# Four row buffers in place of two for the edge pass of a graph network on one core

## The reference, cut to what matters

```python
row, col = edge_index[0], edge_index[1]
h = jnp.concatenate([x[row], edge_attr], axis=1) @ W1 + b1      # one row per edge
mu, var = jnp.mean(h, axis=0), jnp.var(h, axis=0)               # over all edges
h = (h - mu) * jax.lax.rsqrt(var + EPS) * gamma + beta
msg = h * jax.nn.sigmoid(h)
sums = jax.ops.segment_sum(msg, col, num_segments=N)
```

## Time and profile before

| | us |
|---|---|
| median of 3 executions (9289.38 to 9297.74) | 9289.8 |
| the profiled execution: its own time | 9297.53 |
| its span in the trace | 9295.6 |
| edge pass in it, first gather to last add | 1831.93 to 4319.14 |
| mean granted TensorE clock over the span | 0.772 of full |

### The profile page before, as it was taken

One profiled execution on the slowest core, in us unless ns is written; L12 is line 12 of the kernel. 1 busy time (PEld: TensorE's weight loads), 2 busy tenths in 40 slices (PEclk: granted clock), 3 DMA queues, 4 the chain that ended last, 5 costly groups with the idle time before them and its releaser, 6 DMA issues.

```text
span 9295.6 us, 165844 instructions
## 1 busy us (share of the span) xinstructions
PE 5847.5 (63%) x64897; PEld 5071.9 (55%) x64897; DVE 2786.7 (30%) x4913; ACT 1277.2 (14%) x1585; POOL 3571.9 (38%) x3542
## 2 busy tenths in 40 slices
PE   6999899834444444435775345555455545699999
PEld 6999699722222222224765234444444444699998
DVE  6999411100000000003873233333233333311111
ACT  4777400000000000001443000000000000000000
POOL 2111000066666666665531655555555555200000
PEclk9999899866666666667995566666666666899999
DMA  4444188722222222223321122222222222499887
GB/s 128 183 182 183 63 257 256 210 64 68 68 68 68 68 68 66 67 67 82 113 83 28 23 72 71 75 75 75 74 72 74 72 68 75 141 291 290 261 256 227
DMA packets 522673, 1099.41 MB, mean 118 GB/s; under 512 B 150990, under 2 KB 330192, under 8 KB 509440
## 3 DMA queue, kind: packets, MB, share of 16 engines
q1 hardware_dynamic: 216192, 767.24, 26.0%
q10 hardware_dynamic: 197184, 211.90, 7.2%
q0 software_dynamic: 108896, 114.33, 6.2%
HBM read 871.53 MB, written 221.62 MB: 118 GB/s over the span
## 4 chain that ended last, share of the span: by engine, by line
PE 37%; another core or an unknown queue 21%; issue 19%; DVE 4%; POOL 3%; ACT 1%; DMA 1%; DVEq 1%; ACTq 0%; POOLq 0%; SPq 0%; PEldq 0%
PE banks L832 18%; PE banks L928 9%; PE banks L938 5%; POOL gath L333 3%; PE banks L351 2%; PE banks L507 1%; DVE oneh L989 1%; DVE area L1699 1%; DVE area L1727 1%; DMA gath<-tab_l,idx 1%; PE banks L519 1%; ACT gath L1306 1%; PE banks L499 1%; DMA gath<-counts 0%
## 5 line engine op out<-in xcount | busy, mean ns | idle before, releaser
L333 POOL DMA_INDIRECT gath<-tab_l,idx x3328 | 3145.4, 945 | 3443.3 <-DMA idx<-src_idx 1197.0
L1458 PE MATMUL banks<-area,ones 128*128 128x448 f32 (+1 forms) x1040 | 686.8, 834 | 1446.9 <-DVE area L1699 1269.5
L1458 PEld LDWEIGHTS banks<-area,ones 128*128 128x128 f32 x1040 | 310.5, 314 | 1791.4 <-issue 1790.6
L928 PE MATMUL banks<-area 128*128 128x128 f16 x4802 | 577.3, 248 | 890.7 <-issue 889.6
L928 PEld LDWEIGHTS banks<-area 128*128 128x128 fp8e4 x4802 | 358.8, 108 | 1094.0 <-issue 1090.1
L938 PE MATMUL banks<-oneh,gath 128*64 128x128 f32 x3328 | 598.0, 358 | 430.2 <-DMA gath<-tab_l,idx 325.8
L1699 DVE TENSOR_TENSOR area<-gath,banks 128x448 f32<-128x448 f32 (+1 forms) x256 | 138.8, 583 | 2350.3 <-remote 2281.0
L938 PEld LDWEIGHTS banks<-oneh,gath 128*64 128x64 f32 x3328 | 556.1, 191 | 461.1 <-DMA gath<-tab_l,idx 330.8
L792 ACT CAST wide<-banks 128x784 uint16<-128x784 f32 x784 | 650.4, 857 | 223.6 <-PE banks L749 223.6
L761 PE MATMUL banks<-feat,wide 128*128 128x129 f16 x9604 | 671.3, 220 | 0.3 <-ACT wide L792 0.3
L832 PE MATMUL banks<-wide,gath 128*128 128x128 f16 x9604 | 580.0, 224 | 45.2 <-issue 25.1
(11 more groups left out here) (234 smaller groups left out, 6159.2 us busy)
## 6 DMA issues: line engine op xcount, KB each, us to landing
gath<-counts SPq DMA_DIRECT2D x294, 784.0 KB, 4.4
oneh<-counts SPq DMA_DIRECT2D x294, 784.0 KB, 4.5
counts<-wide SPq DMA_DIRECT2D x98, 1568.0 KB, 5.2
gath<-counts ACTq DMA_DIRECT2D x98, 784.0 KB
area<-counts ACTq DMA_DIRECT2D x98, 784.0 KB
area<-edge_feat SPq DMA_DIRECT2D x128, 448.0 KB
gath<-tab_l,idx POOLq DMA_INDIRECT x3328
edge_h<-area ACTq DMA_DIRECT2D x128, 416.0 KB
```

The lines of the kernel that those rows point to most:

```text
L333: pool.indirect_dma_start(out=to[:, h, c, 0:H], out_offset=None, in_=table[:, :], in_offset=bass.IndirectOffsetOnAxis(ap=idx[:, slot, c:c ...
L928: last = T.matmul(to, part_in[u].bitcast(f8)[:, t, s * P:(s + 1) * P], block_rows[:, k % 2, s, :, :].rearrange("p a f -> p (a f)"), start= ...
L1458: ins = T.matmul(bank[n][:, 0:(hi - lo) * H], ones[:, :], src[:, lo:hi, :].rearrange("p c f -> p (c f)"), start=first and lo == 0, stop=la ...
```

## The change: what it does

The same memory (`gath`, 13 KB per partition) is seen in the edge pass as four row buffers without gaps, in place of two with gaps. Each buffer has its own semaphore for landed rows. GpSimd's wait on line 331 becomes one for the add of group q-4. VectorE's loop goes over four groups per turn in place of two, reading from the buffer `slot`; its four waits and two instructions per group are kept. The wait for the list, SyncE's queue with its bounds, TensorE's and ScalarE's code, and all other passes are as they were.

```diff
+        edge_rows = flat_of(gath).rearrange("p (s c f) -> p s c f", s=RING, f=H)
...
-            def __init__(self, name, gathers=True, sums=True):
+            def __init__(self, name, gathers=True, sums=True, slots=2):
                 if gathers:
-                    self.rows_in = sems(f"{name}_rows_in")
+                    self.rows_in = sems(f"{name}_rows_in", slots)
...
-        p_edge, p_msg = Pass("edge", sums=False), Pass("msg", gathers=False)
+        p_edge, p_msg = Pass("edge", sums=False, slots=RING), Pass("msg", gathers=False)
...
-        def gather(pool, p, n_win, windows, table, used, before, to=gath):
+        def gather(pool, p, n_win, windows, table, used, before, to=gath, slots=2):
...
                             slot = 2 * v + h
                             hold(pool, idx_in[slot], 16 * ((first + w) * (ITERS // 2) + j + 1))
-                            hold(pool, used, 2 * (w * ITERS + 2 * j + v) + h + 3)
+                            hold(pool, used, 2 * (w * ITERS + 2 * j + v) + h + RING + 1 - slots)
                             for c in range(C):
                                 pool.indirect_dma_start(
-                                    out=to[:, h, c, 0:H], out_offset=None, in_=table[:, :],
+                                    out=to[:, slot % slots, c, 0:H], out_offset=None, in_=table[:, :],
                                     in_offset=bass.IndirectOffsetOnAxis(ap=idx[:, slot, c:c + 1], axis=0),
-                                ).then_inc(p.rows_in[h], 16)
+                                ).then_inc(p.rows_in[slot % slots], 16)
...
-            gather(pool, p_edge, n_win, 1, tab_l1, s_eh, (before, 0))
+            gather(pool, p_edge, n_win, 1, tab_l1, s_eh, (before, 0), to=edge_rows, slots=RING)
...
-                with dve.Fori(0, ITERS) as i:
-                    for h in range(2):
+                with dve.Fori(0, ITERS // 2) as j:
+                    for slot in range(RING):
+                        h, i = slot % 2, 2 * j + slot // 2
                         q = 2 * i + h
-                        hold(dve, p_edge.rows_in[h], 16 * C * (i + 1))
+                        hold(dve, p_edge.rows_in[slot], 16 * C * (j + 1))
...
-                                ebuf[:, h, lo:hi, :], gath[:, h, lo:hi, 0:H],
+                                ebuf[:, h, lo:hi, :], edge_rows[:, slot, lo:hi, :],
```

## The result

| | before | after |
|---|---|---|
| median, us (4 executions each) | 9289.59 | 9486.85 |
| lowest to highest | 9286.47 to 9297.74 | 9481.76 to 9489.98 |
| ratio | | 1.021, 95% interval 1.0195 to 1.0225 |
| profiled execution: span, us | 9295.6 | 9488.1 |
| edge pass in it, first gather to last add | 2487.2 | 2673.3 |

The change costs 197 us, 2.1%. The forecast was 9,442, so the sign and the kind were right and the size was short by 45 us. The span grew by 192.5 us, and 186.1 of that is the edge pass. Of the 6.4 us outside it 2.1 lie ahead of the pass and the rest behind it.

The account below looks back on a forecast made before the run. Waits, not a full engine, set the edge pass's pace, with TensorE's second count getting through when GpSimd stops. Runs of three, 124 / 3 x 62.1 = 2,567 us, gave +152 on 9,297.5, less 7.7: 9,442 us; range 9,220 to 9,620.

Parts of the forecast that it names:

- The new wait: Edge pass, GpSimd: the list load takes over from the add, restarting gathers 5.9 us after an add, not 0.81.
- The run of three: Edge pass: GpSimd issues three groups per stop, 62.1 us per run, 20.7 per group against 19.43; chance 0.38.
- restart: Edge pass: time from the add's end to GpSimd's next gather, put at 5.9 us, with the list's load.
- The order of the adds: Edge pass: both products nearly through before the run slows TensorE, so both adds of a pair can come in the run.
- The start: Start of edge pass: first run becomes four groups, 64.5 us; add 1 ends at 1904, 16 us later than before.
- gets through only when GpSimd stops: Edge pass: the count of a pair's second product reaches VectorE when GpSimd stops issuing, not after a fixed time.
- The bound with the list in time: Edge pass: restart 0.81 us after the add in place of 5.9, making the kernel 210 us less than the forecast.
- Pairs with the list: Edge pass rival: old two-group cycle plus the list load, 43.96 us per two groups, +311 us, 9,600 us; chance 0.25.
- runs of four: Edge pass: four groups per stop, 19.6 us per group, about +20 us; chance 0.13 shared with the fixed delay.
- runs of five: Edge pass: five groups per stop, 18.9 us per group, −68 us, 9,222 us; longer runs have chance 0.09.
- The fixed delay: TensorE rival: second product done 26 us after its row whatever GpSimd does, no change, 9,290 us; 0.13 with runs of four.
- GpSimd bound: Edge pass rival: gathers never stop, 2,065 us plus about 12 in place of 2,487, −410 us, 8,880 us; chance 0.15.

Follow-up runs that it names:

- run 3: Changed kernel with GpSimd gathering only the first four groups of the edge pass, the other 124 reusing those rows: 7673.76 us.
- run 4: Changed kernel with each edge-pass group's rows fetched by one plain DMA on SyncE's queue, no gathers on GpSimd: 7667.89 us.
- run 8: Changed kernel with each indirect DMA of the edge pass replaced by a plain one of the same size, also from GpSimd: 7773.42 us.
- run 2: Changed kernel with only GpSimd's wait put back to the add of group q-2: 9364.69 us, 0.9999 of the kernel before.
- run 5: Changed kernel with eight list slots, list q+4 loaded once group q-4 has been added: 9365.55 us, 1.0007 of the kernel before.
- run 1: Changed kernel with each source list one place earlier in SyncE's queue, ahead of the previous group's features: 9547.39 us, 1.0193 of the kernel before.
- run 10: Changed kernel with eight list slots and 7 products per group in place of 13, on the third chip: 8054.67 us, 0.9982 of the kernel before.
- run 9: Kernel of run 4 plus the pass's 1,664 indirect DMAs from GpSimd into memory nobody reads, on the third chip: 8027.13 us; kernel before 8068.78.
- run 12: Kernel of run 9 measured again on a fourth chip: 8027.63 us, where the kernel before takes 8067.54.

## Why the prediction was right, and where it was short

**What bounded the kernel.** Right for the chips of the result. Without indirect DMAs a pair takes 12.2 us in place of 38.9, and the products are seen by VectorE at their row's end (runs 3, 4). The counts do depend on GpSimd's issuing, and on its indirect DMAs or the scattered rows that come with them (run 8).

**The new wait.** Right: the list takes over from the add, and alone accounts for the loss (runs 2 and 5). The edit to GpSimd's bound costs 197 us, and with lists in time 0.07%, which the interval doesn't tell from nothing. I had given as reason that list q is queued behind features q-1. Run 1 shows that this isn't needed: with only four list slots the load can't start before GpSimd's own bound.

**The run of three.** Right in count (41 of 43 runs), and the rate nearly so. Forecast: 62.1 us. Measured in the run shown: 48.47 issue + 6.97 to the add + 1.08 add + 6.59 to the restart = 63.1. As a mean from the run that starts at 1933.14 to the one at 4440.30, 120 groups, 62.7, with a restart of 6.45 and 6.67 to the add. The term that was mis-sized most is the restart, 6.45 for 5.9: I had ended it with the burst of traffic, and the list is there only a little behind it. Over these 40 cycles that makes 23 us of the 34 by which the pass (2,673 us) exceeds the forecast's 2,639. The mean stop of 14.0 us is at the end of the 12 to 14 that I had given; most are 14.0 to 14.7.

**The end of the pass.** Not in the sum. The last three groups are gathered in one run, and their adds wait for its end: the last issue ends at 4488.8 and the last add at 4507.2, 18.4 us later, where the kernel before needs 5.1 and the forecast's last run had 6.75 + 1.08 = 7.8. That is 10.6 us more than forecast. With the 23 us of the cycles, 2.5 at the start (below) and 2.1 less because the pass began that much later, it makes up the 34. Of the 45 us by which the median misses, 6.4 more lie outside the pass, and 4.6 come from the step from the profiled execution to the median, 3.1 us here and 7.7 before.

**The order of the adds.** The forecast had both adds of a pair in every run. Two kinds of run alternate, without exception from the first run of three to the next to last. In one, two adds fall in the run and two at its stop: 60 and 61 in the run shown, 62 and 63 after it. In the other, one falls in the run and one at its stop: 64 at 3195.40, and 65 at 3240.20. That is six adds in two cycles. What makes every run three long is the list's bound, which I had right: list 65 stands behind features 64, which wait for the add of 62. The reason that I gave for the adds, that both products of a pair get through early in the run, holds for every second run only; in the others the second product is caught as it was before the change.

**The start.** Forecast: add 1 at 1904, after a run of four. It came at 1889.8, inside that run, 47 us after its products' row and with GpSimd still issuing, which it did to 1898.7. So "gets through only when GpSimd stops" is too strong; "creeps" is the better word, and TensorE's single rows about 2.5 us apart say how fast. The effect on the sum is small: a stop of 3.8 us, a run of one group and a stop of 14.6 us follow, and the first run of three starts with group 5 at 1933.14, where the forecast's line has 1904 + 5.9 + 20.7 = 1930.6.

**The bound with the list in time.** Wrong. I put it at 210 us under the forecast, 9,232, keeping runs of three. Run 5 gave 1.0007, as without the change, in runs of two. The step that failed is that the run's length and the stop's were taken as independent. My reading is that a gather that restarts 0.8 us after the add catches the second product again, while one that restarts after 6.6 us lets more through; no run varies the restart alone. By it the time per group is TensorE's: how much it gets done in a stop and in the first 10 us of a run.

**The rivals.** Pairs with the list (9,600) were excluded by the runs of three. By the prediction's own terms runs of four come to +11 us, not +20, and runs of five to -74, not -68; no chance hangs on that. The fixed delay fell with runs 3 and 4. "GpSimd bound" was false for the result and true on the third chip for the kernel of run 10; the kernel before is 14% faster there. The ratio 1.021 therefore belongs to the first kind of chip. The change was not measured on the other kind.

**Open.** What tells the two kinds of chip apart. Whether it is the indirect form or the scattered rows that slows TensorE. And whether the indirect DMAs alone hold TensorE up on the first kind, or only together with the loop that waits for them: run 9 would have said so, but ran on the other kind. Why TensorE creeps isn't shown by any run. That its rows show some work at full pace first (8 rows of sums and 20 of products in the run shown) and then single ones looks like instructions that arrive late, but no run tests this, and the rows ahead of a wait can't be taken at their word.

## What to carry to other kernels

Before you loosen a wait, look for the next one behind it and ask whether that resource has the same bound: with four buffers and four list slots the list load moved into every stop, and the pass became 7.5% longer. More buffers gave a lead here, not a rate (run 5). First find what sets the rate, here TensorE's pace beside the gathers, and take instructions out of it (0.992 with two buffers). And where an engine's ends are modelled, date its work by the engine that waits for it.

## What the runs showed that I had not expected

- On the first kind of chip TensorE goes down to one matmul row in some 2.5 us while GpSimd issues indirect DMAs, where 52 take 6 us without them; plain DMAs from the same engine at more than twice the rate don't do this (run 8). Some of SyncE's issues stretch too: 0.70 us beside the gathers, and 0.33 in the stop for the same load.

```profile
3138.26 0.70 SPq L321 DMA_DIRECT2D area<-edge_feat  x1
```

- This differs between chips of the same type: the kernel before takes 9,365 and 9,357 us on two (9,290 where the result was taken), and 8,069 and 8,068 on two others. On the latter TensorE isn't slowed by indirect DMAs (runs 9 and 12).
- A wait of some 45 us for a count whose row had ended repeats all through the pass: the add of group 65 comes 46.2 us after its products' row, that of group 125 45.7 us.
